# Depthwise convolution stages of a fused kernel: four accumulators instead of two, and another order of work on ACT and DVE

## What is computed

```python
def _conv_bn(x, w, s, b, groups=1):
    y = lax.conv_general_dilated(x, w, (1, 1), 'SAME', dimension_numbers=('NCHW', 'OIHW', 'NCHW'), feature_group_count=groups)
    return y * s[None, :, None, None] + b[None, :, None, None]

def _ffn(x, w1, s1, b1, w2, s2, b2):
    return _conv_bn(jax.nn.relu(_conv_bn(x, w1, s1, b1)), w2, s2, b2)

x = x + _conv_bn(x, dw0_w, dw0_s, dw0_b, groups=C)      # stage 0: 3x3 depthwise
x = x + _ffn(x, f0_w1, ...)                             # stage 0: 1x1, 64 -> 128 -> 64
x = x + _windowed_attn(x, ...)
x = x + _conv_bn(x, dw1_w, dw1_s, dw1_b, groups=C)      # stage 1
x = x + _ffn(x, f1_w1, ...)                             # stage 1
```

## Time and profile before

| What | Value |
|---|---|
| median of 3 runs | 1367.01 us (1366.44 to 1367.26) |
| profiled execution | 1367.41 us |
| its span | 1365.6 us |
| mean granted PE clock over the span | 0.772 |
| busy over the span: PE, DVE, ACT, POOL | 77%, 62%, 38%, 19% |
| convolution stage of layer 0 | from 7.3 us (first PE work) to the barrier behind 55.8 |
| convolution stage of layer 1 | from 220.4 (first DVE work) to 268.9 |

### The profile page before, as it was taken

The page is one execution under the profiler, slowest core; times in us unless marked ns, Lnnn a source line. Parts: engine busy times, 40 slices in busy tenths (PEclk is TensorE's granted clock), DMA queues, the critical chain, the costliest instruction groups (busy, mean ns, idle before and its releaser), DMA issues. The chain is left out here.

```text
span 1365.6 us, 27455 instructions
## 1 busy us (share of the span) xinstructions
PE 1045.2 (77%) x9710; PEld 611.4 (45%) x9710; DVE 848.6 (62%) x2482; ACT 519.7 (38%) x1338; POOL 264.8 (19%) x375
## 2 busy tenths in 40 slices
PE   6778786767988756666666666666973899999996
PEld 2356652253666535454454545453542333333332
DVE  6586845745556365555555555554346688888885
ACT  3443442453443323232323232223641545554452
POOL 3303012300000000000000000000100255555555
PEclk9898997868999865555555555557985999999998
DMA  6000002000000000000000000000000775555650
GB/s 226 1 1 1 1 2 78 0 1 1 1 0 0 1 1 0 0 0 0 0 0 0 0 0 0 0 0 1 0 1 8 146 149 130 123 123 121 131 117 23
DMA packets 23059, 47.41 MB, mean 35 GB/s; under 512 B 1616, under 2 KB 5840, under 8 KB 22608
## 3 DMA queue, kind: packets, MB, share of 16 engines
q1 hardware_dynamic: 22992, 46.51, 14.7%
HBM read 43.88 MB, written 2.62 MB: 34 GB/s over the span
## 5 line engine op out<-in xcount | busy, mean ns | idle before, releaser
L1613 PE MATMUL wide<-ls_h,ls_v 128*128 128x16 f16 x2304 | 104.1, 176 | 144.4 <-DVE ls_h L1712 141.2
L2115 ACT ACTIVATE ex_gated<-wide,unscale 128x1024 f32<-128x1024 f32 x128 | 142.1, 1113 | 138.8 <-PE wide L2081 138.7
L2131 DVE TENSOR_TENSOR ex_hid<-wide,ex_gated 128x1024 f32<-128x1024 f32 x128 | 156.0, 1223 | 44.5 <-ACT ex_gated L2115 40.0
L1613 PEld LDWEIGHTS wide<-ls_h,ls_v 128*128 128x128 bf16 x2304 | 81.0, 105 | 213.4 <-DVE ls_h L1712 213.4
L2057 POOL TENSOR_TENSOR ex_acc<-ex_part,ex_acc 128x512 f32<-128x512 f32 x120 | 152.3, 1270 | 94.9 <-DVE ex_part L2147 80.7
L1702 DVE TENSOR_TENSOR_SCAN ls_cells<-ls_terms 128x48 f32<-128x48 f32 x256 | 73.6, 288 | 124.1 <-ACT ls_terms L1637 124.1
L1637 ACT ACTIVATE ls_terms<-wide 128x32 f32<-128x32 f32 x256 | 54.4, 213 | 229.6 <-PE wide L1618 229.6
L2093 PE MATMUL wide<-ex_hid,w 128*64 128x512 f32 x512 | 116.7, 598 | 0.0
L2081 PE MATMUL wide<-xh,wh 64*128 64x512 f16 x512 | 98.8, 382 | 4.6 <-PEq L81 3.2
L2081 PE MATMUL wide<-xh,wl 64*128 64x512 f16 x512 | 98.0, 379 | 0.0
L2081 PE MATMUL wide<-xl,wh 64*128 64x512 f16 x512 | 97.8, 378 | 0.0
(11 more groups left out here) (364 smaller groups left out, 1925.4 us busy)
## 6 DMA issues: line engine op xcount, KB each, us to landing
ex_d<-route SPq DMA_DIRECT2D x64, 512.0 KB, 7.9
par_attn<-in_attn SPq DMA_DIRECT2D x1, 2704.0 KB, 13.3
par_rest<-in_rest SPq DMA_DIRECT2D x1, 2539.0 KB, 18.6
L_xin<-in_x SPq DMA_DIRECT2D x8, 256.0 KB, 5.6
w<-in_w SPq DMA_DIRECT2D x1, 2048.0 KB, 7.9
out<-ex_acc SPq DMA_DIRECT2D x16, 128.0 KB, 4.6
w<-in_w SPq DMA_DIRECT2D x1, 512.0 KB, 8.9
route<-ro_dt SPq DMA_DIRECT2D x8, 64.0 KB, 1.7
```

What stands on the lines that cost most here:

```text
L1613: pe.matmul(ig[:, g, :] if g < 2 else o, vp[part][:, g, :], h1[:], start=False, stop=False, skip_group_check=True)
L2115: act.activation(gated[:, n % 2, :], pair_of_up(n // GS, 2 * (n % GS))[:], ACT.Silu, scale=m.unscale[:, 0:1]).then_inc(s["gated_ready"], 1)
L2131: dve.tensor_tensor(hid[:, n % (2 * GS), :], pair_of_up(n // GS, 2 * (n % GS) + 1)[:], gated[:, n % 2, :], ALU.mult).then_inc(s["hid_ready ...
```

## The change

`acc` gets four buffers, chosen by tile number modulo 4. The first tap of a tile waits for DVE's adds of the tile four before it, not two. ACT takes the first taps of pairs 0 and 1 ahead of its loop, and those of pair i + 2 between `hidden(i)` and `ffn_out(i)`. DVE convolves pairs 0 and 1 first, and takes the statistics of pair i - 2 behind the convolution of pair i. Both loops are Python loops, written out in the program. PE's and POOL's programs stay.

```diff
-        acc = sb("acc", [P, 2, 2 * PADW * SIDE])
+        acc = sb("acc", [P, 4, 2 * PADW * SIDE])
...
-        def acc_rows(k):
-            return acc[:, k, 0:(2 * SIDE + 1) * SIDE].rearrange("p (r c) -> p r c", c=SIDE)
+        def acc_rows(t):
+            return acc[:, t % 4, 0:(2 * SIDE + 1) * SIDE].rearrange("p (r c) -> p r c", c=SIDE)
...
-                    act.wait_ge(y_ready, t + 1)
-                    act.activation(acc_rows(k), rows_of(t, 0), ACT.Identity, bias=dw_b[:, 0:1],
+                    if t >= 4:
+                        act.wait_ge(y_ready, t - 1)
+                    act.activation(acc_rows(t), rows_of(t, 0), ACT.Identity, bias=dw_b[:, 0:1],
                                    scale=taps[:, 0:1]).then_inc(acc_ready, 1)
...
             first_tap(0)
-            with act.Fori(0, PAIRS - 1) as i:
-                first_tap(i + 1)
+            first_tap(1)
+            for i in range(PAIRS):
                 hidden(i)
+                if i + 2 < PAIRS:
+                    first_tap(i + 2)
                 ffn_out(i)
-            hidden(PAIRS - 1)
-            ffn_out(PAIRS - 1)
...
-                        dve.scalar_tensor_tensor(acc_rows(k), rows_of(t, q), taps[:, q:q + 1], acc_rows(k),
+                        dve.scalar_tensor_tensor(acc_rows(t), rows_of(t, q), taps[:, q:q + 1], acc_rows(t),
                                                  ALU.mult, ALU.add).then_inc(tap_step, 1)
...
-                    a = acc[:, k, :].rearrange("p (a r c) -> p a r c", a=2, r=PADW)[:, :, 0:SIDE, :]
+                    a = acc[:, t % 4, :].rearrange("p (a r c) -> p a r c", a=2, r=PADW)[:, :, 0:SIDE, :]
...
             conv(0)
-            with dve.Fori(0, PAIRS - 1) as i:
-                conv(i + 1)
-                finish(i)
+            conv(1)
+            for i in range(2, PAIRS):
+                conv(i)
+                finish(i - 2)
+            finish(PAIRS - 2)
             finish(PAIRS - 1)
```

## The result

| | before | changed |
|---|---|---|
| median of 15 runs | 1367.01 us (1358.62 to 1369.21) | 1356.27 us (1354.55 to 1357.6) |
| profiled execution, span | 1367.41, 1365.6 | 1354.55, 1352.8 |
| mean granted clock | 0.772 | 0.777 |

The ratio is 0.9924 (95%: 0.9913 to 0.9936).

The account below looks back on a forecast made before the run. PE, the most loaded engine, was taken to bound the convolution stages, stopping only for DVE's adds. Gains of 0.84 us (first stage) and 2.7 us (second), summed to 3.5 us, gave 1363.5 us; range 1361.2 to 1366.0.

Parts of the forecast that it names:

- Layer 0: 0.84 us, from ACT's first tap: First convolution stage: earlier first taps on ACT let PE start up of pair 2 at 38.53, not 39.37: 0.84 us off.
- What is late next is PE itself: First convolution stage, pair 3: DVE's taps end about 44.6, PE's convolution at 45.8, so no new wait.
- Layer 1: 2.7 us, from the order of the statistics: Second convolution stage: PE's gap and slow clock go, 3.69 us, with 1 us given back to POOL's adds: 2.7 us off.
- Whoever has a run of instructions going keeps the operands until the run ends: Second convolution stage: POOL's adds of pair 0 are put off to 245.8, so up of pair 3 starts at 258.1.
- rival B: Both convolution stages: POOL's adds interleave with DVE's taps, 1.27 us each, two per pair; total 2.2 us, 1364.8 us; chance 0.17.
- I take nothing, either way.: Loops of both convolution stages: their register work does not show in the time, so writing them out counts as nothing.
- 0.84 + 2.7 = 3.5 us: Sum of the gains in the first and second convolution stages, taken off the median 1367.01 us to give 1363.5 us.
- Rival C: Between the convolution stages, four microseconds more or fewer at the lower clock cost or give 1.9 us: 1365.5 or 1361.6; chance 0.14.
- stretches behind the stages that change their length by more than the two stages gain: Profile sign, behind the two convolution stages, that the prediction is wrong altogether; the stages' gain was put at 3.5 us.
- three runs lie within 0.8 us: Whole kernel: argument against a slower result, about 1370 us from slightly over 13 us more at the lower clock, chance 0.05.

Follow-up runs that it names:

- the two filled kernels: Kernel before and changed kernel, each with ten unused matmuls put in PE's 3.03 us wait in slice attention: 1358.82 and 1355.8 us.
- layer 1 only: Kernel before with the whole change in layer 1's convolution stage only: 1358.21 us, ratio 0.9943.
- delayed before: Kernel before plus a POOL memset of 250 columns at the end of layer 1's convolution stage: 1359.95 us, ratio 0.9964.

## Why the prediction was wrong, step by step

**Layer 0: 0.84 us, from ACT's first tap.** Right in mechanism, a little large. Up of pair 2, counted from the first matmul, came at 38.96 - 7.54 = 31.42 instead of 32.11, 0.69 us earlier; up of pair 3 at 40.75 instead of 41.25, 0.50 earlier. The difference is the taps of pair 3, 8.91 us long, which end at 47.6 where I had 44.6: PE starts up 0.19 us behind its own work. "What is late next is PE itself" was wrong by this much. The loops have no part in it: with them written out and nothing else, the gap ahead of pair 2 is still there (0.76 us).

**Layer 1: 2.7 us, from the order of the statistics.** Right in size and in what went: gap and slow clock, 3.69 us as worked out from the earlier trace rows, less a new gap of 0.74 us, 2.95 measured. But the order of the statistics made only about half of it. From 39.24 us, writing out the loops leads to 38.02, the order of the statistics on top of that to 36.49, and all the rest to 36.29. The granted clock, 227 to 256 us in the changed kernel, is 1.00 through the new gap:

```profile
227.00:256.00 29.00, 28.26 (x88) 10.29 (x89) 29.00 (x43) 15.88 (x22) 7.17 (x6) 1.00 0.00 1
```

**"Whoever has a run of instructions going keeps the operands until the run ends": failed.** I had POOL's adds of pair 0 put off to the end of the taps. They began when they were ready and ended 3.03 us later (3.02 in layer 0), with two taps stretched to 1.8 us beside them: rival B's picture, single taps of 2 us among the ten. It is also what the Trainium skill says ("SBUF — State Buffer", section "Who interferes with whom"): the shared pair of ports is held for one whole instruction, and this case's trace now agrees, with taps of 1.78 and 1.80 us; only the 2.41 us POOL add of the earlier trace rows, overtaken by a tap, still speaks against it. The price per add was 1.03 us, not rival B's 1.27, and POOL's adds of pair 1, from 245.21 us, fell mostly beside the four statistics, so the last ten taps took 7.54 us. The end, a gap of 0.74 instead of 0.96 us, came out near for another reason than mine: that was luck.

**Loops written out: "I take nothing, either way."** Right for the total (1367.24 us), wrong for layer 1: the gap shrinks by 0.35 us and the clock no longer falls behind it, 1.2 us of the 2.95. Counted from the first matmul, DVE was done with the adds of pair 1 0.23 us earlier, and began the taps of pair 2 0.35 us earlier; the distance of taps inside one pass, from which the prediction argued, says nothing of what stands between the passes.

**The sum, "0.84 + 2.7 = 3.5 us", and behind it nothing.** This is the step that failed. The stages gave 3.44 us in the profile and 3.0 us between the two filled kernels, as forecast. But the sum ended at the last edited stage. Rival C had the mechanism, "The gain is made and partly eaten behind the stage" and "It can also give", and gave it 1.9 us either way, from four microseconds at the lower level in the attention stage. It was priced from the clock of one stretch, 54.5 to 220.4 us; no gap of PE behind 269 us entered it. The trace of before had the one that mattered: 3.03 us ahead of `sl_bm` in the last tile but one of slice attention, with matmuls behind it at 3.78 and 3.36 us where 1.99 and 2.01 are their time at full clock. Reading it would have given rival C a one-sided price: this stage was already paying 5.5 us, which the change could only hand back. That is a case at 1363.5 - 5.5 = 1358.0, and the range had to reach below it. The prediction's own sign of being wrong altogether, "stretches behind the stages that change their length by more than the two stages gain", came: 5.59 us against 3.44.

The range was too narrow on one more count: the 15 runs of before reach from 1358.62 to 1369.21 us, where the three that the argument "three runs lie within 0.8 us" used did not. Such a spread on one program is larger than the edit's gain.

**What stays open.** What exactly decides whether the clock falls behind the gap was not settled. The length of layer 1's stage is not enough (36.37 and 36.49 us go apart), nor is the start of the stage. In the profiled executions that kept the clock without a filler (changed, layer 1 only, delayed before), the whitening ahead took 47.8 to 47.9 us up to its norm; in those that lost it, 48.2 to 49.4. That is a coincidence of rows, and no run tests it. The 1.24 us between LSTM and experts go with slice attention: in all 14 profiled executions that stage takes 132.4 to 133.1 us where slice attention kept the clock and 133.8 to 134.4 where it lost it. It begins at the lower level in both kernels, for 5.6 us before (928.19 to 933.8) and for 3.8 us changed (916.81 to 920.6). Why the two go together was not tested.

## What to carry to other kernels

Before a small gain is added up, look in the whole trace for places where PE waits for a few microseconds and the same matmuls are slower behind the wait than elsewhere: each is a sum of its own that a shift in time can give or take, here 5.5 us against 3.4 from the edit. To tell what an edit is worth, read the edited stage from its own first instruction to its last, or fill such a wait with matmuls in both kernels, and do not trust the total alone: a delay of under half a microsecond made this kernel 6.5 us faster. Even a filled wait did not make the total additive here. Do not count written-out loops as nothing, either: 0.35 us less in a wait was worth 1.2 us of the stage. Where DVE's two-operand instructions and POOL's adds overlap, each POOL add of 1.3 us costs DVE about 1.0 us; it is paid only if DVE comes out behind PE.

## What the runs showed of the hardware that was not expected

- The same wait of 3.03 us, behind the same matmuls, is followed by the full clock (1.99 us for eight, granted 0.97 over the stage) in one kernel and by the lower level (3.78 us, 0.92) in another. The length of this wait alone does not tell. Behind 1.98 us, in layer 1 before, the clock fell as well (2.79 us against 1.99), in each of the four kernels that have this wait; behind 1.63 us, in two other kernels, it did not.
- The lower level came back. It held for 10.2 us, the clock was full for 3.3 us, and then low again for 3.3 us: 17.59 us at a mean granted clock of 0.64 from the end of the gap to the next stage.
- Ten matmuls without use (20 records, 2.40 us of PE) came with a time 7.6 us shorter, 5.5 us of it in the stage in which they stand.
- POOL and DVE took turns by single instructions: taps 0.77, then 1.80 and 1.78 us, and POOL's second add 1.76 instead of 1.3 us.
